# Scores of two heads in one exponential, and projections in the maxima's ring of banks

## The reference

```python
for c in range(6):
    q = ew[c, 0] * (nodes[in_q] @ We[eq] + be[eq])
    k = ew[c, 1] * (nodes[in_k] @ We[ek] + be[ek])
    v = ew[c, 2] * (nodes[in_v] @ We[ev] + be[ev])
    o = _mha(q, k, v, Wq[c], Wk[c], Wv[c], Wo[c])
    nodes[c] = act_w[c] * o + q
out = layernorm(nodes[5]) * ln_g + ln_b
```

## Time and profile before

| | us |
|---|---|
| median of 3 runs (2580.66 to 2599.03) | 2598.49 |
| profiled execution | 2587.72 |
| its span, first to last instruction | 2585.9 |
| PE busy | 2319.4 |
| DVE busy | 2235.8 |
| ACT busy | 1781.2 |
| POOL busy | 115.0 |

### The profile page before, as it was taken

One profiled execution on the slowest core, in us unless ns is written; L12 is line 12 of the kernel. 1 busy time (PEld: TensorE's weight loads), 2 busy tenths in 40 slices (PEclk: granted clock), 3 DMA queues, 4 the chain that ended last, 5 costly groups with the idle time before them and its releaser, 6 DMA issues.

```text
span 2585.9 us, 39227 instructions
## 1 busy us (share of the span) xinstructions
PE 2319.4 (90%) x13473; PEld 869.1 (34%) x13473; DVE 2235.8 (86%) x3998; ACT 1781.2 (69%) x3417; POOL 115.0 (4%) x74
## 2 busy tenths in 40 slices
PE   6588989999999999999999999999999999999996
PEld 3233333333333333333333333333333333333331
DVE  7488788899989999899999999999899899898982
ACT  3136567777777777777777777777777777767773
POOL 1000000000000000000000000000000000010110
PEclk8679899999999999999999999999999999999995
DMA  3404133242253243253243243243243243143311
GB/s 90 108 21 83 39 74 79 54 115 77 60 114 75 62 114 76 61 115 80 58 114 81 57 105 85 46 105 83 47 105 87 44 105 89 42 104 88 65 29 33
DMA packets 93262, 198.46 MB, mean 77 GB/s; under 512 B 26115, under 2 KB 43799, under 8 KB 93063
## 3 DMA queue, kind: packets, MB, share of 16 engines
q1 hardware_dynamic: 93062, 195.96, 32.4%
HBM read 116.65 MB, written 64.42 MB: 70 GB/s over the span
## 4 chain that ended last, share of the span: by engine, by line
PE 63%; DVE 14%; ACT 11%; DMA 6%; issue 4%; SPq 2%; ACTq 0%; POOL 0%; POOLq 0%; DVEq 0%
PE bank L511 25%; PE bank L464 22%; ACT e_ring L670 10%; DVE max_half L963 9%; PE bank L484 5%; DMA q_aug<-max_part 5%; PE bank L312 2%; PE bank L323 2%; PE bank L342 2%; SPq L1167 2%; PE bank L331 1%; PE bank L257 1%; PE bank L350 1%; ACT raw L680 1%; PE bank L258 1%
## 5 line engine op out<-in xcount | busy, mean ns | idle before, releaser
L963 DVE TENSOR_REDUCE max_half<-bank 128x1 f32<-128x512 f32 x3072 | 1924.3, 682 | 257.1 <-PE bank L484 243.4
L670 ACT ACTIVATE e_ring<-bank 128x512 f32<-128x512 f32 x3072 | 1610.9, 601 | 609.7 <-PE bank L464 609.4
L464 PE MATMUL bank<-q_aug,k_aug 50*128 50x512 f32 x3072 | 1142.0, 453 | 159.0 <-ACT e_ring L670 149.7
L484 PE MATMUL bank<-k_aug,q_aug 48*128 48x512 f32 x3072 | 1153.0, 456 | 48.2 <-DMA q_aug<-part_dram 25.7
L464 PEld LDWEIGHTS bank<-q_aug,k_aug 50*128 50x128 f32 x3072 | 503.2, 188 | 1209.9 <-ACT e_ring L670 1113.0
L511 PE MATMUL bank<-e_ring,v_aug 128*32 128x512 f32 x6144 | 836.7, 617 | 0.0
L484 PEld LDWEIGHTS bank<-k_aug,q_aug 48*128 48x128 f32 x3072 | 500.8, 188 | 84.9 <-DVE max_half L963 49.6
L511 PEld LDWEIGHTS bank<-e_ring,v_aug 128*32 128x32 f32 x6144 | 121.7, 108 | 206.4 <-ACT e_ring L670 117.9
L1030 POOL TENSOR_TENSOR ctxT<-ctxT,rden_bc 128x1024 f32<-128x1024 f32 x23 | 54.6, 2375 | 1938.9 <-DMA rden_bc<-rden_dram 1938.8
L680 ACT ACTIVATE raw<-bank 128x512 f32<-128x512 f32 x96 | 57.4, 598 | 27.9 <-PE bank L511 26.0
L331 PE MATMUL bank<-node_ring,w_q 128*128 128x512 f32 x96 | 56.2, 670 | 3.1 <-DVE k_part L805 0.7
(11 more groups left out here) (167 smaller groups left out, 687.8 us busy)
## 6 DMA issues: line engine op xcount, KB each, us to landing
part_dram<-k_part SPq DMA_DIRECT2D x24, 1024.0 KB, 4.0
k_aug<-part_dram SPq DMA_DIRECT2D x48, 512.0 KB, 10.1
part_dram<-q_part SPq DMA_DIRECT2D x24, 1024.0 KB, 5.0
q_aug<-part_dram SPq DMA_DIRECT2D x48, 512.0 KB, 13.4
src<-node_dram SPq DMA_DIRECT2D x40, 512.0 KB, 3.4
k_aug<-part_dram SPq DMA_DIRECT2D x48, 256.0 KB, 8.1
q_aug<-part_dram SPq DMA_DIRECT2D x48, 256.0 KB, 14.4
q_aug<-max_part SPq DMA_DIRECT2D x768, 2.0 KB
```

Source lines behind the costliest of these rows:

```text
L464: e.matmul(bank[i][:, :], k_aug[first:first + AUG, u % 2, h // 2, chunk * P:(chunk + 1) * P].bitcast(F32R), q_aug[first:first + AUG, u % 2 ...
L484: e.matmul(bank[i][:, :], q_aug[first:first + SPLIT, u % 2, h // 2, q0:q0 + P].bitcast(F32R), k_aug[first:first + SPLIT, u % 2, h // 2, ha ...
L670: e.activation(e_ring[:, n % E_SLOTS, :], bank[i][:, :], ACT.Exp, scale=EXP_SCALE).then_inc(a_exp, 1)
L963: e.tensor_reduce(max_half[:, G % 2, row, kh:kh + 1], bank[MAX_BANKS[ring % 3]][:, :], AX_X, ALU.max).then_inc(v_mx, 1)
```

## The change

Scores of two heads (a *pair*) go to two neighbouring banks, `score0` (banks 0 and 1) or `score1` (banks 2 and 3), and one exponential of 1024 columns reads both. `e_ring` has five slots of 1024. The weights times v come two steps later instead of one (`PV_LAG`), and between the two pairs of a step. The context bank is 7. Banks 4, 5 and 6 form one ring for the maxima, their transposes and all projections and mixing products; a bank is free when the reader of its last content has signalled. GpSimd makes both parts of q and k from an fp32 copy that ACT writes to SBUF (a copy to fp32r, then the difference); `rest_k` and `rest_q` on DVE are gone. Evictions of the projections stand one step later, behind the first exponential of that step, and `store_q`, `load_aug` and the reciprocals are one or two steps later.

```diff
-        ST_BANKS, MAX_BANKS, CTX_BANK, MISC = (0, 1, 2), (3, 4, 5), 6, 7
+        score = [ctx.enter_context(nc.psum_tensor(f"score{i}", [P, 2 * BANK], F32)) for i in range(2)]
+        RING, CTX_BANK = (4, 5, 6), 7
...
+            def next_bank():
+                ring[0] += 1
+                return RING[ring[0] % len(RING)]
...
+            def scores(s, pair):
+                n = 2 * s + pair
+                if n >= 2:
+                    e.wait_ge(a_exp, n - 1)
...
+                if pair == 0 and chunk == 0:
+                    e.wait_ge(d_max_in[G % 2], DMA * 2 * HG * (G // 2 + 1))
+                for j in range(2):
+                    done = e.matmul(bank[2 * pair + j][:, :], ...)
+                done.then_inc(p_st, 1)
+
+            def maxima(m):
+                i = where["mx", m] = next_bank()
+                bk = free_bank(i)
...
+                freed[i] = (v_mx, m + 1)
...
             for s in range(-LOOKAHEAD, LAST_STEP):
+                for pair in range(2):
+                    if 0 <= s < STEPS:
+                        scores(s, pair)
+                    for m in range(HG * (s + LOOKAHEAD) + 2 * pair, HG * (s + LOOKAHEAD) + 2 * pair + 2):
+                        if m < GROUPS * NCH * HG:
+                            maxima(m)
+                    if pair == 0:
+                        if 0 <= s - PV_LAG < STEPS:
+                            weighted(s - PV_LAG)
+                        G = (s + LOOKAHEAD - 2) // NCH
+                        if s % NCH == 3 and 0 <= G < GROUPS:
+                            turn_maxima(G)
+                        for i, k in late_stages(s):
+                            mix(i, k, next_bank)
+                stages(s)
...
@@ scalar_program
+                if 0 <= s < STEPS:
+                    weights(s, 0)
+                stages(s - 1)
...
+                    evict_context(G)
+                if 0 <= s < STEPS:
+                    weights(s, 1)
+                for i, k in late_stages(s):
+                    mix(i, k)
...
+                e.activation(e_ring[:, n % E_PAIRS, :], score[pair][:, :], ACT.Exp, scale=EXP_SCALE).then_inc(a_exp, 1)
...
@@ vector_program
                 for j in range(HG):
                     m = HG * (s + LOOKAHEAD) + j
                     if m < GROUPS * NCH * HG:
+                        maxima(m)
                     if j % 2:
+                        stages(s - 1, j // 2)
+                    if j == 2 and s % NCH == 3 and 0 <= G < GROUPS:
+                        split_maxima(G)
+                for i, k in late_stages(s):
+                    mix(i, k)
...
@@ gpsimd_program
+            def split(part, hf, signal_to):
+                x, high = part[:, 1, half_of(hf)], part[:, 0, half_of(hf)]
+                step(e.tensor_copy(high.bitcast(F32R), x))
+                signal(e.tensor_tensor(x, x, high, ALU.subtract), signal_to)
...
@@ sync_program
-                        if k == 8:
-                            store_q(nxt)
                         if k in (8, 9):
                             load_aug(nxt, 1, k - 8)
-                        if k in (11, 12):
-                            load_aug(nxt, 0, k - 11)
+                        if k == 10:
+                            store_q(nxt)
+                        if k in (12, 13):
+                            load_aug(nxt, 0, k - 12)
```

More of the change, by code:

```diff
@@ L19 @@
 LOOKAHEAD = 14
-E_SLOTS = 10
+E_PAIRS = 5
+PV_LAG = 2
 Q_SLOTS = (0, 1, 0)
@@ L597, in last_turn, with stages @@
                     e.wait_ge(d_out, DMA * (B - 1))
-                e.activation(last_y[:, half_of(hf)], bank[MISC][:, :], ACT.Copy).then_inc(a_last, 1)
-            def stages(s, half):
+                e.activation(last_y[:, half_of(hf)], bank[where["lt", hf]][:, :], ACT.Copy).then_inc(a_last, 1)
+            def stages(s):
                 u, r = divmod(s, UC)
@@ L899, in stages @@
                 if 0 <= prev < LAST:
-                    if half == 0 and r == 5:
+                    if half == 0 and r == 6:
                         e.wait_ge(d_den_in, DMA * (prev + 1))
@@ L1079, in gpsimd_program @@
                     mix(i, k)
+                z = t - UNIT0_AT
+                if z == 1:
+                    for hf in range(NHALF):
+                        split_k(0, hf)
+                if z == 3:
+                    for hf in range(NHALF):
+                        split_q(0, hf)
             e.wait_ge(p_mt2, EARLY)
```

382 lines of the change are left out of this document (175 added, 207 removed).

## The result

The changed kernel takes 2973.3 us, median of three runs (2960.2, 2973.3 and 3001.7); the kernel before takes 2598.8, median of four from 2580.7 to 2599.2. A fourth run of the changed kernel took 3012.1 us in a slower state (over 1.5% above its fastest run) and is counted neither in this median nor in the ratio; with it the median would be 2987.5. The ratio is 1.148, with a 95% interval of 1.136 to 1.160: slower, as forecast, and inside the range of 2760 to 3020, but 83 us above the forecast of 2890. The profiled execution took 2960.2 (span 2958.4), 372.5 more than the 2587.7 of before, where the sum had put +304.

The account below looks back on a forecast made before the run. The prediction took the PE-DVE maxima's loop as the bound; 231 for 21 units, 22 and 26 for units 0 and 1, 6 and -12 for unit 23, and 31 of stalls gave +304 on 2588: 2890 us, range 2760 to 3020.

Parts of the forecast that it names:

- the sum: Whole kernel: longer units, first and last units and stalls add +304 us to the profiled 2588, giving 2890.
- the maxima's loop: PE and DVE's reductions, through three banks, set each plain step, which goes from 2.74 to 2.97 us.
- The rival on the other side: ACT's loop sets plain steps, which shrink to 2.54 us: 2560, or 2450 with less at projections; chance 0.07.
- The projections: Waits for bank readers add 0.8 us six times a unit where ACT reads, 1.27 four times where DVE reads.
- The transpose: A longer way to the scores and a wait for its reader add 0.79 us, four times a unit: 3.2.
- The wait at step 16: Scores of step 16 wait for the maxima's DMAs: a stall of 1.4 us a unit, bounds 0 and 5.
- the rival with 0.16: PE's clock halves after stalls at step 16, 29 us more: 2920; also around transposes, 134 more: 3050; chance 0.16.
- The rest of the rival: Thinner steps around each transpose also lose the clock: 96 x 1.4 = 134 us more, 3050; within the chance 0.16.
- the forecast's unit of 109.5 us: Forecast length of one steady unit, stall at step 16 included, against 97.1 us before.
- It counts as nothing: GpSimd's split removes some 2.8 us a unit of DVE time, not on the path, so no gain is credited.
- forecast 48: Units 0 and 1: 22 us for the longer units and 26 for mixing products holding up the maxima's ring.
- the forecast's 12: Last 14 steps of unit 23, without maxima: between nothing and 27 us gained, put down as -12.

Follow-up runs that it names:

- Experiment 7: Kernel before, with PE making both scores of a pair ahead of both maxima, all else unchanged: 2698.2 us, ratio 1.037.
- experiment 1: Changed kernel with tiles in the order score, maximum, score, maximum within each pair: 2961.0 us, ratio 1.139.
- experiment 5: Changed kernel with a maximum between the scores only in the second pair, and only if the step before had no projection: 2966.3 us, ratio 1.142.
- 8: Changed kernel with the tile order of experiment 5, the maxima's DMAs ahead of q's loads, and the transpose one step earlier: 2814.1 us, ratio 1.083.
- 9: Kernel 8 with projection evictions ahead of the step's first exponential and first reduction, and the split ahead of the third reduction: 2629.0 us, ratio 1.012.
- experiment 10: Kernel 9 with the mixing products' readers also moved, ahead of ACT's second exponential and DVE's third reduction: 2577.2 us, ratio 0.9926.
- experiment 3: Changed kernel with two exponentials of 512 columns in place of each one of 1024: 3025.0 us, ratio 1.162.
- experiment 12: Changed kernel with only projection evictions ahead of the first exponential and first reduction, and the split ahead of the third reduction: 2770.3 us, ratio 1.071.
- 2, SP's old order: Changed kernel with q's store ahead of k's loads and q's loads one step earlier: 3089.3 us, ratio 1.186.
- 4, 1 and 2: Changed kernel with maxima between the scores of each pair and SP's order of before: 2994.7 us, ratio 1.155.
- 6, maxima's DMAs first: Changed kernel with q's store ahead of k's loads and q's loads behind the eight DMAs of the maxima: 2911.0 us, ratio 1.120.
- experiment 11: Kernel before with GpSimd's split alone, ACT writing an fp32 copy of k and q: 2574.2 us, ratio 0.9922.

## Why the prediction was right, and where it was off

**What bounds.** Right. The prediction said that the maxima's loop and not ACT's work sets the step, and that the loop goes from 2.74 to 2.97; it is 2.94. Experiment 7 makes the same 2.94 in the old kernel by the order alone, and experiment 1 takes it back to 2.71 by the order alone; 5, 8, 9 and 10, which have this order in the second pair, also show 2.71 and 2.72. The rival on the other side, ACT's loop as the true one, falls: ACT's waits grew by 477 us, and experiment 3 gives ACT its second instruction back without a move in the plain steps.

**The projections.** Right in mechanism and near in size: behind one that ACT reads 3.74 (forecast 3.74 to 3.86, counted as 3.77), behind one that DVE reads 4.19 (forecast 4.24). The prediction put 9.9 us a unit on these; experiment 12 takes most of the wait for the readers away, and the unit falls by 8.4, some of it by the clock and by the split's new place. It is the largest single cause. The prediction had the eviction "behind an exponential" and "two reductions" in its terms; it didn't say that this place is a choice, worth more than half of the loss.

**The transpose.** Off by a little. The terms were added as if a transpose and a projection never met. They do, at steps 2 and 3 and at 26 and 27, as a chain of three waits; the two stretches came out 0.5 us each above the forecast.

**The wait at step 16.** The chain was the one described, q's store behind k's loads, then loads, then the eight small DMAs. Each piece was near: the store took 11.86 us, and the wait came 21 times with 1.9 us where 1.4 was forecast. The term "22 x 1.4 = 31" was mis-sized by this, 39.0 for 31, and by what it left out, the halved clock behind a wait, which the prediction had only as a rival.

**The clock.** This was the rival with 0.16, and a good part of it came true; it is what the sum left out. The mean grant fell from 0.959 to 0.939. In units 2 to 21 the kernel before has 17 us at a grant of 0.50, the changed one 160. Of the 21 waits at step 16, 16 were followed by it. The rest of the rival, the clock lost around the transposes, happened at the meetings with projections: at steps 3 and 4 in 5 of the 20 units, and behind step 27 in 8 of them; behind the other two transposes the clock fell once. What it costs can be read there, from the same steps of one kernel: steps 26 to 28 take 12.7 us in twelve units at full clock and 13.8 or 13.9 in the eight others, steps 2 to 4 take 11.9 against 13.4 to 13.7 with one such stretch and 14.5 with two. Steps 26 to 28 of units 9 and 10 of the changed kernel (busy us of PE, PEld, DVE, ACT, POOL, then PEclk, DMA share, GB/s):

```profile
1339.48:1352.15 12.67, 9.99 (x65) 4.65 (x65) 8.97 (x17) 6.15 (x7) 0.00 (x0) 1.00 0.05 12
1456.98:1470.83 13.85, 11.49 (x65) 5.14 (x65) 9.30 (x18) 6.04 (x7) 0.00 (x0) 0.88 0.05 13
```

For each kernel I set the length of each of the 20 units against its halved clock and put a straight line through; its value at zero says how long a unit would be at full clock. This is an estimate, from one execution of each kernel (in experiments 1 to 5 no unit ran wholly at full clock); a longer wait at step 16 also goes with more halved clock, so the slope (0.28 to 0.39 us for each us at the halved clock) holds a little of the wait too.

| kernel | unit, us | halved clock in it | wait at step 16 | unit by the line, without halved clock |
|---|---|---|---|---|
| changed | 113.2 | 8.0 | 1.9 | 110.0 |
| 1, maxima between | 112.3 | 12.6 | 2.2 | 108.7 |
| 2, SP's old order | 119.2 | 20.9 | 3.9 | 112.0 |
| 3, two exponentials | 117.2 | 18.3 | 2.0 | 110.3 |
| 4, 1 and 2 | 114.2 | 13.6 | 4.4 | 110.0 |
| 5, between, second pair | 114.4 | 19.5 | 3.1 | 107.3 |
| 6, maxima's DMAs first | 111.0 | 6.1 | 0 | 108.8 |
| 12, readers first alone | 104.8 | 5.6 | 2.1 | 102.7 |

So the forecast's unit of 109.5 us was nearly that of the changed kernel at full clock: its two units without halved clock took 109.3 and 109.5. Of the 3.7 us that it was short, some 3 are the clock, about 60 us in the whole; the longer waits and the meetings are the rest. The table also says why experiment 5 gained so little: without halved clock its unit is 2.7 us shorter with 1.2 more of waiting, which is the 3.8 that was expected. The prediction's ground for the rival was one wait of 1.39 us; in the same trace waits of 1.47 and 1.59 us at the same step kept the clock, so a wait of this length makes its loss possible and not certain. The median lies 13 us above the profiled run, which had the highest clock of the changed kernel's runs; the prediction put its sum down "unchanged for the median".

**GpSimd.** The cost was right: hidden. "It counts as nothing" was wrong: experiment 11 is 0.8% [0.5%, 1.1%] ahead, inside the 1% that the prediction called no change, but clear of nothing; some 17 us of it stand in units 0 to 21. Steps 4, 6 and 7, where DVE had made the low parts, went from 2.94, 3.56 and 2.87 to 2.74, 3.39 and 2.74. DVE wasn't full on average, but its instructions there stood between two reductions that the ring waited for; this reading of the medians is an argument, not a run. PE's own waits for the low parts, before the second product of k and of q, went at the same time (21.4 us in the whole kernel before, none in this one), and no run parts the two.

**Ends.** Units 0 and 1 cost 45 us more (forecast 48), and the start of step 0 came 5.4 later (163.4 against 158.0). The tail gained more than the forecast's 12: its last 14 steps took 51.0 us in the kernel before (five near 2.7 and nine near 4.1 at the halved clock, where the prediction took all 14 at 4.0) and take 29.7 now, some 22 less; about 9 of these are steps of 2.1 in place of 2.7 at full clock, and 13 are the clock. Against the profiled execution: 21 x 16.1 = 338, + 45, + 5, - 22, which is 366 of the 372.5.

**Open.** Why one kernel has more halved clock than another at equal waits (experiment 3 above all); no run holds the clock fixed, so its price is an estimate. And what the single exponential brings of its own in the steady part of experiment 10: no run has that order with two exponentials, and all that is shown is the 1.0 us of the last 14 steps in experiment 3.

## What to carry to other kernels

When users with different readers are put into one ring of buffers, the ring moves at the pace of the slowest reader, and that pace is mostly its place in the reader's queue: look up what stands ahead of each eviction, and put evictions first. Here it was worth 203 of 375 us, more than the order of the tiles or the DMAs. Time saved on an engine off the loop that binds gives nothing back: ACT's busy time fell by 95 us, and no plain step got shorter. And a gain in the loop can be hidden by the next wait and by the halved clock behind it until these are mended too, so look at the clock's row before an edit is called useless, and try edits together (experiment 5 gave 7 us alone, within the noise; with 6 and the earlier transpose it gave 97 more than 6 alone).

## What the runs showed of the hardware that was not expected

Short waits can cost twice. In the changed kernel PE works without a long pause, but waits at step 16 went with a stretch at a grant of 0.50, within or behind them, in 16 of 21 cases (waits of 0.96 to 3.6 us), and waits of 1.28 us for the split's reader, in a row as at step 27, in 13 of 40. Behind the wait of 1.53 us v's eight products went from 1.0 to 1.74 us. The outcome isn't fixed by the wait alone: after 1.18 us in one unit the clock stayed, and in the kernel before waits of 1.47 and 1.59 us kept it and one of 1.39 didn't. Steps 26 to 28, with the same work, took 1.1 us more where the clock was halved. On the other side, 20 us within the last 14 steps ran at a grant of 1.00, where the kernel before had 0.50 in nine of its own last steps, with the same products. What kept the clock there was not tried.

An exponential of 1024 columns over two banks takes 1.023 us, and two of 512 take 1.03 in a row of four: there is next to no fixed part to be saved in a row of exponentials, only the 0.17 us that two lone ones of 0.60 cost more. Where ACT has hardly any idle time, in the last 14 steps, the long form gave 1.0 us of 30.7.
